# A long tile's probabilities turned by DMA in every third job, low halves of inputs split on GpSimd, and two orders changed

## The reference

```python
def ln(x): return (x - mean(x)) / sqrt(var(x) + 1e-5)        # over the last axis
# x, ctx: (4, 1024, 1024) f32; 16 heads of 64
x = x + causal_attention(q=ln(x), k=ctx, v=ctx)               # scores * 64**-0.5, softmax, @ v
soft   = sigmoid(pweight) - sigmoid(nweight)                  # (1024, 1024, 4)
weight = einsum('oin,n->oi', soft, exps * sigmoid(mask_weight)) * scale
bias   = bit_ste(einsum('on,n->o', pbias - nbias, bexps), 4) * biasscale
x = x + einsum('bsi,oi->bso', ln(x), weight) + bias
```

## Time and profile before

| | |
|---|---|
| median of 3 runs | 1277.42 us (1277.39 to 1278.48) |
| the profiled execution, its own time | 1274.72 us |
| its span in the trace | 1272.9 us |
| PE, DVE, ACT, POOL busy | 92%, 81%, 73%, 47% of the span |
| TensorE clock granted, mean | 0.983; 1.00 in the long tiles' windows |
| DMA queue of SP | 47.2% of 16 engines |

### The profile page before, as it was taken

One profiled execution on the slowest core, in us unless ns is written; L12 is line 12 of the kernel. 1 busy time (PEld: TensorE's weight loads), 2 busy tenths in 40 slices (PEclk: granted clock), 3 DMA queues, 4 the chain that ended last, 5 costly groups with the idle time before them and its releaser, 6 DMA issues.

```text
span 1272.9 us, 29189 instructions
## 1 busy us (share of the span) xinstructions
PE 1166.4 (92%) x11376; PEld 883.3 (69%) x11376; DVE 1034.5 (81%) x1593; ACT 928.5 (73%) x2019; POOL 597.1 (47%) x717
## 2 busy tenths in 40 slices
PE   0677788999999999999999999999999999999998
PEld 0666675677777677777776677787786677777763
DVE  4576677888898888888897888888988888888872
ACT  2688876777877777787777777777787787777750
POOL 3399865433324954433325853333237844332241
PEclk9888899999999999999999999999999999999999
DMA  8979843543224955433316764444326755220112
GB/s 220 305 242 309 296 133 80 127 98 79 68 84 82 203 133 123 90 90 70 97 51 138 166 144 102 103 82 100 67 68 150 169 131 117 67 68 19 35 34 66
DMA packets 228984, 152.92 MB, mean 120 GB/s; under 512 B 204272, under 2 KB 204272, under 8 KB 228848
## 3 DMA queue, kind: packets, MB, share of 16 engines
q1 hardware_dynamic: 227264, 148.92, 47.2%
q10 hardware_dynamic: 1584, 2.14, 0.5%
HBM read 67.15 MB, written 16.78 MB: 66 GB/s over the span
## 4 chain that ended last, share of the span: by engine, by line
PE 63%; DVE 15%; POOL 6%; issue 5%; ACT 5%; DMA 4%; SPq 2%; ACTq 1%; POOLq 0%
PE ffnb L399 19%; PE ptb L367 15%; PE oacc L381 7%; PE slot L354 7%; PE slot L355 7%; DVE pt_lo L561 5%; PE oacc L383 4%; DVE stats L575 4%; POOL v L758 3%; ACT pt_hi L461 2%; DVE mx L554 2%; PE slot L358 2%; DVE ring L610 1%; ACT osb L468 1%; DMA yt<-in_L_ffn_nweight_dram 1%
## 5 line engine op out<-in xcount | busy, mean ns | idle before, releaser
L561 DVE SCALAR_TENSOR_TENSOR pt_lo<-ptb,pt_hi 128x384 f16<-128x384 f32 (+2 forms) x688 | 382.8, 597 | 119.7 <-ACT pt_hi L461 117.5
L461 ACT ACTIVATE pt_hi<-ptb 128x384 f16<-128x384 f32 (+2 forms) x688 | 326.4, 527 | 166.2 <-PE ptb L367 165.5
L451 ACT ACTIVATE p<-slot,mx 128x512 f32<-128x512 f32 (+7 forms) x512 | 378.5, 748 | 52.1 <-DVE mx L554 50.0
L399 PE MATMUL ffnb<-wt,yt 128*128 128x512 f16 x1464 | 371.0, 379 | 19.7 <-DVE ring L610 17.9
L554 DVE TENSOR_REDUCE mx<-slot 128x1 f32<-128x640 f32 (+7 forms) x352 | 359.4, 1021 | 21.3 <-PE slot L358 18.6
L367 PE MATMUL ptb<-id,p 128*128 128x128 f32 x2304 | 323.7, 279 | 11.1 <-DVE pt_lo L561 10.0
L354 PE MATMUL slot<-kt,qt 128*128 128x128 f16 (+3 forms) x1056 | 270.5, 286 | 32.6 <-DMA qs<-qt 28.0
L743 POOL TENSOR_TENSOR att<-osb 128x256 f32<-128x256 f32 x128 | 99.1, 774 | 421.9 <-ACT osb L468 397.7
L355 PE MATMUL slot<-kt,qs 128*128 128x128 f16 (+3 forms) x1056 | 270.0, 285 | 0.0
L367 PEld LDWEIGHTS ptb<-id,p 128*128 128x128 f32 x2304 | 246.3, 141 | 18.2 <-issue 15.7
L381 PE MATMUL oacc<-v,pt_hi 128*128 128x128 f16 x2304 | 244.2, 220 | 3.6 <-DVE pt_lo L561 1.9
(11 more groups left out here) (78 smaller groups left out, 1064.6 us busy)
## 6 DMA issues: line engine op xcount, KB each, us to landing
ring<-in_x_dram SPq DMA_DIRECT2D x32, 512.0 KB, 4.9
cin<-in_ctx_dram SPq DMA_DIRECT2D x32, 512.0 KB, 4.0
qs<-qt SPq DMA_DIRECT2D x64, 256.0 KB, 3.9
out_dram<-ring SPq DMA_DIRECT2D x32, 512.0 KB, 2.9
v<-in_L_ffn_pweight_dram SPq DMA_DIRECT2D x20, 512.0 KB, 7.0
kt<-in_L_ffn_nweight_dram SPq DMA_DIRECT2D x15, 512.0 KB, 7.7
kt<-in_L_ffn_pweight_dram SPq DMA_DIRECT2D x5, 512.0 KB, 5.1
ring<-in_L_ffn_pweight_dram SPq DMA_DIRECT2D x5, 512.0 KB, 5.4
```

The costliest lines, as they stand in the source:

```text
L399: last = pe.matmul(dst, yt[:, k % 2, a * KT_N + kk, :], wt[:, c, kk, half * 512:half * 512 + 512], start=r == 0, stop=r == 3 * KT_N - 1)
L451: last = nc.scalar.activation(p32[:, j.par, hh * j.keys:(hh + 1) * j.keys], slot[:, j.par, base:base + j.keys], ACT.Exp, bias=mx[:, j.par, ...
L461: nc.scalar.activation(pt_hi[:, j.par, P * blocks.start:P * blocks.stop], ptb[:, c % 2, 0:P * len(blocks)], ACT.Copy, scale=P_SCALE).then_ ...
L561: nc.vector.scalar_tensor_tensor(pt_lo[:, j.par, cols], ptb[:, c % 2, 0:P * len(blocks)], P_SCALE, pt_hi[:, j.par, cols], ALU.mult, ALU.su ...
```

## The change

Jobs of long tiles with q % 3 == 2 (s = 2, 5, 8, 11 and 14, so 5 of 16, 80 in all) are "turned by DMA": ACT copies the float32 probabilities to float16 in a new buffer `p16` (one, not two), DVE subtracts for the low half, SP issues one DMA transpose of 2(i+1) blocks into `pt`, and PE makes no transposes for this job. `pt` holds what `pt_hi` and `pt_lo` held. In tiles with t > 3 and more than 4 steps (22 tiles) y_split, c_split and q_split move from DVE to POOL. On DVE the linear adds go ahead of the y moments. SP asks for the swap at s = 1 in place of s = 0.

```diff
+        self.d = turned if self.heads == 1 and q % 3 == 2 else None
+        count = -(-blocks // 4) if self.d is None else 0
...
+def low_on_pool(t):
+    return t > 3 and steps(t) > 4
...
+            def turn_p(j):
+                sp.wait_ge(p16_lo, j.d + 1)
+                reached(sp, pv_done, j.n - 1)
+                sp.dma_start_transpose(pt[:, j.par, 0:2 * j.blocks], p16[:, 0:2 * j.keys]).then_inc(pt_in, 16)
...
                 for s in range(n):
+                    if JOBS[FIRST[t] + s].d is not None:
+                        turn_p(JOBS[FIRST[t] + s])
                     if s == 0:
                         if t >= 4:
                             store(t - 4)
-                        if t + 1 < TILES:
-                            swap_q(t + 1)
+                    if s == 1 and t + 1 < TILES:
+                        swap_q(t + 1)
...
             def values(j):
-                pe.wait_ge(lo_done, j.chunks[-1][0] + 1)
+                if j.d is None:
+                    pe.wait_ge(lo_done, j.chunks[-1][0] + 1)
+                else:
+                    pe.wait_ge(pt_in, 16 * (j.d + 1))
...
             def exponentials(j):
                 act.wait_ge(mx_ready, j.n + 1)
+                if j.n > 1 and JOBS[j.n - 2].d is not None:
+                    act.wait_ge(p16_lo, JOBS[j.n - 2].d + 1)
...
+                if j.d is not None:
+                    act.wait_ge(p_done, j.n + 1)
+                    reached(act, pt_in, 16 * j.d)
+                    nc.scalar.activation(p16[:, 0:j.keys], p32[:, j.par, 0:j.keys], ACT.Copy, scale=P_SCALE
+                                         ).then_inc(p16_hi, 1)
...
+            def low_part_unturned(j):
+                dve.wait_ge(p16_hi, j.d + 1)
+                nc.vector.scalar_tensor_tensor(p16[:, j.keys:2 * j.keys], p32[:, j.par, 0:j.keys], P_SCALE,
+                                               p16[:, 0:j.keys], ALU.mult, ALU.subtract).then_inc(p16_lo, 1)
...
                     maxima(JOBS[j.n + 2])
+                if j.n + 1 < len(JOBS) and JOBS[j.n + 1].d is not None:
+                    low_part_unturned(JOBS[j.n + 1])
...
-                for k in y_begun(t, s):
-                    y_moments(k)
                 for k, m0, m1 in matmuls_at(t, s):
                     for half in range(2):
                         if m0 < MATMULS // 2 * (half + 1) <= m1:
                             result(k, half)
+                for k in y_begun(t, s):
+                    y_moments(k)
...
+            def c_split(t):
+                pool.wait_ge(c_hi, t + 1)
+                v = v16[:, t % V_PLACES]
+                nc.gpsimd.tensor_tensor(v[:, :, D:2 * D], cin[:, :].rearrange("p (h d) -> p h d", d=D),
+                                        v[:, :, 0:D], ALU.subtract).then_inc(c_lo, 1)
```

More of the change, by code:

```diff
@@ L44, with __init__ @@
 class Job:
-    def __init__(self, n, t, q, chunk0):
+    def __init__(self, n, t, q, chunk0, turned):
         self.n, self.t, self.q = n, t, q
@@ L53, in __init__ @@
         self.par = n % 2
-        blocks = self.heads * (self.i + 1)
-        count = -(-blocks // 4)
-        size = -(-blocks // count)
+        self.blocks = blocks = self.heads * (self.i + 1)
+        self.d = turned if self.heads == 1 and q % 3 == 2 else None
+        count = -(-blocks // 4) if self.d is None else 0
+        size = -(-blocks // count) if count else 0
         self.chunks = [(chunk0 + c, range(size * c, min(size * c + size, blocks))) for c in range(count)]
@@ L66 @@
     for _q in range(H // HPJ[_t % NT]):
-        JOBS.append(Job(len(JOBS), _t, _q, JOBS[-1].chunks[-1][0] + 1 if JOBS else 0))
+        JOBS.append(Job(len(JOBS), _t, _q, sum(len(j.chunks) for j in JOBS), sum(j.d is not None for j in JOBS)))
 FIRST.append(len(JOBS))
@@ L166, in build @@
         ring = sb("ring", [P, RING, DM], F32)
-        spare32 = sb("spare32", [P, DM], F32)
+        p16 = sb("p16", [P, 2 * 8 * P], F16)
         cin = sb("cin", [P, DM], F32)
@@ L362, in transpose_p @@
             def transpose_p(j):
-                pe.wait_ge(p_done, j.n + 1)
+                if j.d is None:
+                    pe.wait_ge(p_done, j.n + 1)
                 for c, blocks in j.chunks:
@@ L460, in high_parts @@
                     act.wait_ge(t_done, c + 1)
-                    nc.scalar.activation(pt_hi[:, j.par, P * blocks.start:P * blocks.stop],
-                                         ptb[:, c % 2, 0:P * len(blocks)], ACT.Copy, scale=P_SCALE
-                                         ).then_inc(hi_done, 1)
+                    nc.scalar.activation(pt[:, j.par, blocks.start:blocks.stop, :],
+                                         ptb[:, c % 2, 0:P * len(blocks)].rearrange("p (k c) -> p k c", c=P),
+                                         ACT.Copy, scale=P_SCALE).then_inc(hi_done, 1)
             def output(g):
@@ L680, in _ @@
                     weights_sum(j.n + 1)
[L681 to L684, removed]
+                if not low_on_pool(t):
+                    for k in y_at(t, s, 2):
+                        y_split(k)
+                    if s == C_LO[steps(t)] and t + 2 < TILES:
+                        c_split(t + 2)
                 if q_at(t, s, 0):
                     q_moments(t + 2)
-                if q_at(t, s, 3):
+                if not low_on_pool(t) and q_at(t, s, 3):
                     q_split(t + 2)
-                for k in y_begun(t, s):
-                    y_moments(k)
                 for k, m0, m1 in matmuls_at(t, s):
@@ L784, in _ @@
                     difference(2 * j.n + 3)
+                if low_on_pool(t):
+                    for k in y_at(t, s, 2):
+                        y_split(k)
+                    if s == C_LO[steps(t)] and t + 2 < TILES:
+                        c_split(t + 2)
+                    if q_at(t, s, 3):
+                        q_split(t + 2)
                 if q_at(t, s, 1):
```

28 lines of the change are left out of this document (18 added, 10 removed).

## The result

The changed kernel takes **1309.5 us** (median of 4 runs, 1309.0 to 1312.9), the one before 1277.5 us: ratio 1.0254, interval 1.0236 to 1.0272. It is 32 us slower where 20 less were forecast, and outside the range.

What follows compares the result with a forecast made beforehand. PE was taken to bound the long tiles. -60 - 15 - 8 - 4 + 6 + 50 + 11 = -20 took the profiled 1274.7 us to 1254.7, or 1257 as median, with an 8-in-10 range of 1212 to 1298 us.

Steps and rivals of the forecast that it cites:

- The transposes, -60: On PE: 520 transposes of 0.116 us each go, counted whole because PE sets the time: 60 us less.
- ACT: nothing: On ACT: two copies from PSUM replaced by one of the same columns, with 10 us to spare in a tile: no cost.
- the low part as +11 of contention: On DVE: low parts reading two SBUF buffers collide with POOL, 0.7 us a tile: +11 us, bounds 0 and 38.
- rival 3: DVE and POOL exclude each other completely, meeting a turn in each tile: +38 instead of +11, 1289 us; chance 0.10.
- The turn at s = 8, +50: On SP, behind the context load delayed by POOL's split: PE stands 3.5 us on average over 16 tiles; +50 us taken.
- The new path, +6: From a turn's issue to PE's values: turns about just in time, a few late; bounds 0 and +34, +6 us taken.
- rival 2: A turn costs its 4.4 us whatever its blocks, so shorter tiles' turns come late: 1291 us; chance 0.20.
- DVE, -15 and -8: PE's waits on DVE: adds ahead of moments save 15 us, splits moved off DVE save 8 us before transposes.
- The swap, -4: On SP in the weights' stage: swap at s = 1 lets weights go out earlier; bounds +3 and -7, -4 us taken.
- The first: Rival 1: all turns are in time, or PE's wait at s = 8 is taken up elsewhere: 1207 us; chance 0.20.

Runs made afterwards that it cites:

- the mended kernel: The changed kernel with the swap asked for at s = 0 and the context load of long tiles at s = 9: 1270.8 us, ratio 0.9958.
- e16_no_copies: The mended kernel with its 80 DMA turns and their waits, but without ACT's copies and DVE's low parts in all but four of the 80 jobs: 1244.6 us.
- e14_no_dma: The mended kernel without the 80 DMA turns and the waits for them; ACT's copies and DVE's low parts stay: 1254.0 us, ratio 0.9841.
- e18b_low_only: The kernel of e14_no_dma with DVE's low part kept in all 80 jobs and ACT's copy in only 4: 1230.9 us, ratio 0.9662.
- e19_low_after: The mended kernel, complete, with DVE's low part of a turned job behind the low halves of the job in work: 1321.0 us, ratio 1.0366.
- e7_order_only: The kernel before with one change, the linear adds ahead of the moments on DVE: 1277.5 us, ratio 1.0021.

## Why the prediction was wrong

The forecast was 20 us less, and 32 us more were measured. The step that failed most is the one that priced what replaces the transposes: ACT's copy at nothing and DVE's low part at +11, where they cost 38.5 us without the turns. The steps from the kernel before to the changed one, each from two neighbouring runs: order and splits without turned jobs -5.5; transposes gone -54.0; copy and low part +38.5; turns and waits, with the context load out of the way, +17.1; the context load ahead of the turn at s = 8 +25.2; the late swap +10.7; in all +32.0. Beside the prediction's terms:

- **The transposes, -60.** Right in size: PE's busy time falls by 60.3 us where nothing takes their place, and the time by 54. The chunks on ACT and DVE are gone there too (and the context load is at s = 9), so what the transposes give by themselves was not measured.
- **"ACT: nothing" and the low part as +11 of contention.** This is the step that failed most: 38.5 us. I set the new instructions against the chunks that they replace and compared busy totals, which did not rise, and did not follow the order. Even so counted, with chunks and transposes gone and copy and low part in their place, the exchange gave 15.5 us where -60 and +11 make 49. The copy stands ahead of the high halves and the next exponentials on ACT, the low part ahead of low halves and add on DVE, in a row, in a step that has become shorter by the transposes that are gone. The exponentials of the job after next wait for the low part too.
- **The contention itself.** Of the 80 low parts 55 took their quiet time (at least 0.81, 0.95, 1.08 and 1.22 us for 640 to 1024 columns), 25 took longer, up to 2.93 us, and in all 25 an instruction of POOL was under way when they began: the bias add 11 times, the normalisation 8, a split 6. Of the 55 only nine had one, with less than 0.2 us left. In 24 of the 25 the excess is what was left of that instruction, less some 0.15 us; in the last (830.02, where 0.06 us of the bias add was left) it is the split that followed at 830.03. The whole excess is 110.2 us less 81.2, so 29 us of DVE's time, where I took 11; my bound of 38 was for one turned job of each tile only. That was rival 3's mechanism, and the median of 1216 ns for the y_split misled me: it told how often those two met, not how often a new instruction would. The Trainium skill, SBUF — State Buffer, section Who interferes with whom, has the rule of exclusion between a DVE instruction with two SBUF inputs and a GpSimd instruction that reads SBUF; this trace agrees at every one of the 25 places. How much of the 38.5 us it makes is open: no run here took POOL's normalisation and bias add out of the way, which are 19 of the 25.
- **The turn at s = 8, +50.** The mechanism was right in each link (POOL's split, load, turn, landing 4.6 us). In tile 20 the turn landed 15.0 us after the scores of step 5, which end at 814.2, where I had 15.2; PE came to it after 11.9 us and not 10.1, having waited 0.64 us for `osb` and 0.57 us for the add on the way, so it stood 3.2 us and not 5.1. In all it cost 25 us, some 12 of these by the clock, which no term of mine had; PE's wait for turns was 40.7 us in all, not 65. Nor had I the wait of ACT's copy for the turn before, in the one buffer: 23.1 us in 16 places, of which 8.8 are left in the mended kernel.
- **The new path, +6.** Lone turns landed in 3.3 us for 10 blocks and 4.2 for 16, close to the 3.4 and 4.4 worked out, so rival 2 is refuted. Yet the turns cost 17 us in the mended kernel, with 19.1 us of PE's waits. A late low part is not needed for it: `e16_no_copies` has 23.7 us of such waits with 76 of the 80 low parts left out. The longest wait there is one where the turn stands behind a swap in SP's queue; what makes the others late is open.
- **DVE, -15 and -8.** Order alone +2.2, splits alone (with the swap where it was) -7.1, together -5.5. With the order alone, PE's wait moved from the add to the low halves and `osb`. In the changed kernel, order gave 6 us.
- **The swap, -4.** Wrong in sign, +11. I had the row: SP's queue showed when the weights go out. I had also named the swap's place behind 2 MB of weights, but bounded it at +3 without working out when it lands: 9.8 us after its issue instead of 3.5 for tile 2, and PE starts a tile with it.
- **Rivals.** The first (no late turns) did not hold; the third gave the right side, by an effect that was there (29 us of DVE's time) but whose share of PE's time is open. None of them held the 1309 us, as all terms but one fell short on the same side: transposes by 6 us, their replacement by 27.5, DVE by 17.5, the swap by 14.7, the new path by 11.1; only the turn at s = 8 was 24.8 us cheaper than I had it.

What the copy and the low part cost is shown by `e14_no_dma` to `e18b_low_only` as an amount. That it is by their place in the two orders is read from the chain at 1239 us and, at one more place, at 1250 us; the one run that moved the low part (`e19_low_after`) only exchanged one wait for another. What the 17 us of the turns are made of beyond PE's waits was not taken apart.

## What to carry to other kernels

Work taken off the busiest engine pays only if what replaces it is not in the order of the next engines' queues ahead of what the busiest one needs next: follow the replacement down each queue to the wait that it delays, with the step already shortened, rather than compare totals. Ask of each moved transfer when it lands and not only when it is issued. When the wait for an add was taken away by order alone, nearly as much came back at other waits (`e7_order_only`): look for them before counting the gain.

## What the runs showed of the hardware

- PE's stand of 3.24 us at s = 8 in tile 20 was followed by a stretch at 1.2 GHz (0.67 of full clock over the 5.2 us from 829.3), which lost 1.7 us, half as much again; over the kernel 17 us. The same followed a wait of 2.81 us in `e14_no_dma`, where PE waits for the add in a tile with i = 7 and a low part takes 2.91 us beside POOL's split:

```profile
915.18 2.91 DVE L586 SCALAR_TENSOR_TENSOR p<-p 128x1024 f16<-128x1024 f32 x1 [0.25 <-ACT p L473]
```

```profile
919.60:924.50 4.90, 4.56 (x32) 3.46 (x33) 2.72 (x4) 2.73 (x4) 0.04 (x1) 0.65 0.05 17
```

- A lone DMA turn landed in 3.3 us with 10 blocks and in 4.2 us with 16; in tile 20, the one right behind a context load of 0.5 MB took 1.3 us more than the lone ones.
- A low part with two SBUF inputs on DVE that met an instruction of POOL took its quiet time and what was left of POOL's, less some 0.15 us (24 of the 25 places; at the 25th it was POOL's next instruction).
- The split on POOL took 2.1 to 2.5 us for 1024 columns (means 2133, 2422 and 2545 ns by kind), about twice DVE's 1.21 us, and yet the kernel gained 6 to 7 us by it.
